# Gate of the next batch in a period's last part, slots at its end, statistics behind VectorE's chain, no adds between the dispatch scatters

## The reference

```
scores = softmax(x @ gate_w.T) + gate_b           # 16 experts in 4 groups of 4
keep the 2 groups with the largest sum of their 2 best scores
idx = the 2 best experts in these groups;  weights = softmax values at idx
y = sum over the 2 of weight * ((silu(x We1 + be1) * (x We3 + be3)) We2 + be2)
```

## Time and profile before

| | |
|---|---|
| time, three runs | 1450.14, 1455.86, 1465.67 us; median 1455.86 |
| profiled execution | 1444.71 us; span from first to last instruction 1443.0 us |
| mean granted TensorE clock | 0.943 |
| TensorE busy | 1248.3 us (87%) |
| VectorE busy | 923.5 us (64%) |
| GpSimd busy | 698.3 us (48%) |
| ScalarE busy | 668.2 us (46%) |
| chain that ended last | PE 67%, DVE 11%, issue 7%, ACT 5%, DMA 4%, another core or an unknown queue 3%, POOL 3% |

### The profile page before, as it was taken

How to read it: one execution, slowest core, us unless ns; L and a number is a source line. 1 busy time by engine, 2 the same in 40 slices (tenths; PEclk the granted TensorE clock), 3 DMA queues, 4 the chain that set the end, 5 groups by cost and what they waited for, 6 DMA issues and landing times.

```text
span 1443.0 us, 27088 instructions
## 1 busy us (share of the span) xinstructions
PE 1248.3 (87%) x7150; PEld 991.9 (69%) x7150; DVE 923.5 (64%) x3310; ACT 668.2 (46%) x1466; POOL 698.3 (48%) x848
## 2 busy tenths in 40 slices
PE   4998999899999877999999988979869999999830
PEld 3566665699998756878878874646535899998720
DVE  4674856377876556667766646756734677775556
ACT  3344431477776523344434434434411777775500
POOL 2456766488887430000000003467664688885400
PEclk9997999999999997999999998999989999999965
DMA  9521224555554423111110001122224555554389
GB/s 360 184 72 71 78 86 124 156 159 164 158 161 131 131 90 105 59 60 59 58 48 28 1 0 38 56 86 79 71 90 126 149 161 161 159 158 123 92 325 374
DMA packets 92938, 172.78 MB, mean 120 GB/s; under 512 B 17368, under 2 KB 60141, under 8 KB 91507
## 3 DMA queue, kind: packets, MB, share of 16 engines
q1 hardware_dynamic: 63318, 92.98, 21.7%
q0 software_dynamic: 26016, 67.81, 13.2%
q10 hardware_dynamic: 3456, 10.25, 1.8%
HBM read 88.51 MB, written 86.39 MB: 121 GB/s over the span
## 4 chain that ended last, share of the span: by engine, by line
PE 67%; DVE 11%; issue 7%; ACT 5%; DMA 4%; another core or an unknown queue 3%; POOL 3%; SPq 0%; DVEq 0%; ACTq 0%; POOLq 0%
PE bank L576 18%; PE bank L586 9%; PE bank L444 8%; PE bank L460 6%; PE bank L567 4%; PE bank L620 4%; PE bank L609 4%; PE bank L421 3%; PE bank L683 3%; DMA w<-routed_rows 3%; POOL expert_rows L1388 2%; PE bank L588 2%; PE bank L411 2%; ACT xn L853 1%
## 5 line engine op out<-in xcount | busy, mean ns | idle before, releaser
L1416 POOL DMA_INDIRECT routed_rows<-xn,rdest x286 | 282.9, 989 | 137.0 <-DVE rw L1213 77.3
L576 PE MATMUL bank<-rows,att 128*128 128x128 f32 x2288 | 306.8, 278 | 0.1
L576 PEld LDWEIGHTS bank<-rows,att 128*128 128x128 f32 x2288 | 282.4, 194 | 0.8 <-ACT att L841 0.4
L1388 POOL DMA_INDIRECT expert_rows<-rows,slots x192 | 186.9, 974 | 176.2 <-DVE slots L1005 110.3
L1224 DVE SCALAR_TENSOR_TENSOR rows<-bank,tile_b,att 128x128 f32<-128x128 f32 x286 | 100.1, 350 | 155.5 <-ACT att L846 121.3
L841 ACT COPY att<-w 128x512 f32 x286 | 177.9, 622 | 23.2 <-issue 16.5
L586 PE MATMUL bank<-w,rows 128*128 x572 | 173.3, 385 | 16.4 <-DVE rows L1224 15.4
L460 PE MATMUL bank<-ws,work 128*128 128x256 f32 x512 | 143.6, 424 | 25.3 <-DVE work L1135 15.5
L840 ACT COPY rows<-bank 128x256 f32<-128x256 f32 x286 | 106.7, 373 | 78.3 <-PE bank L567 57.8
L460 PEld LDWEIGHTS bank<-ws,work 128*128 128x128 f32 x512 | 103.2, 211 | 53.9 <-DVE work L1135 20.2
L1375 POOL TENSOR_TENSOR rstd<-ve,minus_half 128x8 f32<-128x8 f32 x8 | 13.1, 1640 | 257.3 <-DVE ve L965 257.3
(11 more groups left out here) (184 smaller groups left out, 2185.6 us busy)
## 6 DMA issues: line engine op xcount, KB each, us to landing
rows<-expert_rows SPq DMA_DIRECT2D x286, 130.5 KB
rows<-routed_rows SPq DMA_DIRECT2D x32, 512.0 KB, 4.2
w<-routed_rows SPq DMA_DIRECT2D x10, 1024.0 KB, 18.6
out<-xres ACTq DMA_DIRECT2D x16, 512.0 KB, 7.2
xres<-in_x SPq DMA_DIRECT2D x7, 1024.0 KB, 9.4
rows<-routed_rows SPq DMA_DIRECT2D x6, 1024.0 KB, 15.2
expert_rows<-pad SPq DMA_DIRECT2D x47, 130.5 KB
routed_rows<-xn,rdest POOLq DMA_INDIRECT x286
```

The lines of the kernel that those rows point to most:

```text
L576: last = nc.tensor.matmul(rh_ps[t % RB][:, n * P:(n + 1) * P], m.rw13[:, t % RB, c * C + n * INTER:c * C + (n + 1) * INTER], m.rT[:, t % R ...
L1388: nc.gpsimd.indirect_dma_start(out=d.xg, out_offset=bass.IndirectOffsetOnAxis(ap=m.slots[:, b % XS, k, i:i + 1], axis=0), in_=xs[:, i, :], ...
L1416: nc.gpsimd.indirect_dma_start(out=d.yt, out_offset=bass.IndirectOffsetOnAxis(ap=m.rdest[:, n:n + 1], axis=0), in_=m.ry[:, n, :], in_offse ...
```

## The change

`FIRST` becomes (0, 2, 7, 12, 17, 22, 27, 32, 37): period 0 has two parts, each later one five. The gates of batch r + 1 stand in the last part of period b (behind part 1 for period 0), and the rank matmuls of batch r in the middle of that part. The transposes move up: one in the period's second part, two in the third, one in the fourth. The gates wait for the transposed half they read instead of for both. VectorE's chain stands first in the period, the statistics of batch r + 2 behind it, then slots of batch r, the last part's work, and `negate_mean(r + 2)`. ScalarE makes the exponentials before it normalises. GpSimd makes no add among the dispatch scatters and no longer waits for `y_added` there; `rstd(r + 3)` stands behind both scatters, except `rstd(10)` in layer 1's first period. All 128 adds of a layer follow the DMAs of tiles 0 to 127 in the expert stage.

```diff
-FIRST = (0, 5, 9, 14, 18, 23, 27, 32, 37)
+FIRST = (0, 2, 7, 12, 17, 22, 27, 32, 37)
...
-BIAS_PARTS = [(b, i, c) for b in reversed(range(BATCHES)) for i in range(NT) for c in (0, P)
-              if b >= BATCHES - 2 or i >= 4 or c]
...
                 if i == 0:
-                    pe.wait_ge(s.xT_copied, 4 * r + 4)
                     wait(pe, s.shift_ready, r)
+                if i % PAIRS == 0:
+                    pe.wait_ge(s.xT_copied, 4 * r + 2 + 2 * (i // PAIRS))
...
                     if b == 0:
                         if L == 0:
                             gate_tiles(r, range(NT))
-                        shared(L, n)
-                        shared(L, n + 1)
+                        shared(L, 0)
+                        shared(L, 1)
                         for j in range(4):
                             transpose(r + 1, j)
                         rank(r)
-                        for j in range(n + 2, FIRST[1]):
-                            shared(L, j)
+                        gate_tiles(r + 1, range(NT))
                         continue
-                    shared(L, n, gate_pair)
-                    shared(L, n + 1)
-                    shared(L, n + 2, first_half)
-                    shared(L, n + 3, second_half)
-                    if n + 4 < FIRST[b + 1]:
-                        shared(L, n + 4)
-                    rank(r)
+
+                    def transposes(at):
+                        return lambda j: transpose(r + 1, at[j]) if more and j in at else None
+
+                    def gates(j):
+                        if more:
+                            gate_tiles(r + 1, (2 * j, 2 * j + 1))
+                        if j == 1:
+                            rank(r)
+
+                    n = FIRST[b]
+                    shared(L, n)
+                    shared(L, n + 1, transposes({1: 0}))
+                    shared(L, n + 2, transposes({1: 1, 3: 2}))
+                    shared(L, n + 3, transposes({1: 3}))
+                    shared(L, n + 4, gates)
...
-                    if more:
+                    if b == 0:
                         normalise(r + 1)
-                    if b == 0:
                         exponentials(r)
...
+                    exponentials(r)
+                    if more:
+                        normalise(r + 1)
                     shared(L, n)
-                    exponentials(r)
                     shared(L, n + 1)
...
-                    if n + 4 < FIRST[b + 1]:
-                        shared(L, n + 4)
                     meta(r)
+                    shared(L, n + 4)
...
             def route_work(r):
                 b = r % BATCHES
-                if b > 1:
-                    yield from slots(r - 1)
-                if b + 2 < BATCHES and r != BATCHES:
+                if r == 0:
                     yield from stats_work(r + 2)
...
-                if b + 2 < BATCHES and r != BATCHES:
+                if r == 0:
                     negate_mean(r + 2)
-                yield
+                elif b + 2 < BATCHES and b:
+                    yield from stats_work(r + 2)
...
                         if L:
                             for _ in stats_work(r + 2):
                                 pass
-                        for j in range(n + 2, FIRST[1]):
-                            shared(L, j, iter(()), 0)
                         if L:
                             negate_mean(r + 2)
                         continue
-                    shared(L, n, work, (3 if b > 1 else 0) + (5 if b + 2 < BATCHES else 0) + 1)
-                    others = FIRST[b + 1] - n - 1
-                    for j in range(others):
-                        shared(L, n + 1 + j, work, 17 // others + 1)
+                    shared(L, n, work, 6)
+                    for j in range(1, 4):
+                        shared(L, n + j, work, 5)
                     for _ in work:
                         pass
+                    for _ in slots(r):
+                        pass
+                    shared(L, n + 4, iter(()), 0)
+                    if b + 2 < BATCHES:
+                        negate_mean(r + 2)
...
                 xs = m.xs[b % XS]
-                if b >= 2 and k == 0:
-                    pool.wait_ge(s.y_added, PAIRS * (r - 1))
...
-                    if b >= 2 and i % 4 == 3:
-                        add_bias((b - 2, 2 * k + i // 4, 0))
...
                     if r == BATCHES:
                         rstd(r + 2)
-                    elif b + 3 < BATCHES:
+                    scatter(r, 1)
+                    if b + 3 < BATCHES:
                         rstd(r + 3)
-                    scatter(r, 1)
-                    if r == BATCHES:
-                        rstd(r + 3)
+
+            def add_bias(L, i):
+                if i >= 2 * NT * BATCHES:
+                    return
+                if i == 0:
+                    pool.wait_ge(s.y_added, PAIRS * (BATCHES * L + 7))
+                b, j = (BATCHES - 1 + i // (2 * NT)) % BATCHES, i % (2 * NT)
...
+                if i in (2 * NT - 1, 2 * NT * BATCHES - 1):
+                    last.then_inc(s.bias_added, 1)
```

More of the change, by code:

```diff
@@ L508, in route @@
                     more = b + 1 < BATCHES
-                    def gate_pair(j):
-                        gate(r, 2 * j)
-                        gate(r, 2 * j + 1)
-                    def first_half(j):
-                        if more and j % 2 == 0:
-                            transpose(r + 1, j // 2)
-                    def second_half(j):
-                        if more and j % 2 == 0:
-                            transpose(r + 1, 2 + j // 2)
-                    n = FIRST[b]
                     if b == 0:
@@ L1081, in route_work @@
                 yield
-                if b + 2 < BATCHES and r != BATCHES:
+                if r == 0:
                     negate_mean(r + 2)
-                yield
+                elif b + 2 < BATCHES and b:
+                    yield from stats_work(r + 2)
             def table_work(L):
-                yield from slots(BATCHES * L + BATCHES - 1)
                 nc.vector.tensor_copy(m.pad_to[:], m.carry[:]).then_inc(s.pads_ready, 1)
@@ L1375, in a_rstd @@
                 nc.gpsimd.tensor_tensor(m.rstd[:], m.ve[:], m.minus_half[:], ALU.pow).then_inc(s.a_rstd_ready, 1)
-            def add_bias(part):
-                b, i, c = part
-                x = m.xres[:, b, i, c:c + P]
-                return nc.gpsimd.tensor_tensor(x, x, m.half_bs2[:, c:c + P], ALU.add)
             def scatter(r, k):
@@ L1402, in route @@
                         rstd(r + 2)
-                    elif b + 3 < BATCHES:
+                    scatter(r, 1)
+                    if b + 3 < BATCHES:
                         rstd(r + 3)
-                    scatter(r, 1)
-                    if r == BATCHES:
-                        rstd(r + 3)
+            def add_bias(L, i):
[4 more added lines that the diff above has]
+                b, j = (BATCHES - 1 + i // (2 * NT)) % BATCHES, i % (2 * NT)
+                c = j % 2 * P
+                x = m.xres[:, b, j // 2, c:c + P]
+                last = nc.gpsimd.tensor_tensor(x, x, m.half_bs2[:, c:c + P], ALU.add)
+                if i in (2 * NT - 1, 2 * NT * BATCHES - 1):
+                    last.then_inc(s.bias_added, 1)
             def experts(L):
@@ L1419, in experts @@
                         bounds_check=last_row, oob_is_err=False).then_inc(s.rows_out[n], 16)
-                    if i == 0:
-                        pool.wait_ge(s.y_added, PAIRS * (BATCHES * L + 7))
-                    if i < len(BIAS_PARTS):
-                        last = add_bias(BIAS_PARTS[i])
-                    if i in (2 * NT - 1, len(BIAS_PARTS) - 1):
-                        last.then_inc(s.bias_added, 1)
+                    add_bias(L, i)
             ch.did(nc.gpsimd.memset(m.minus_half[:], -0.5))
```

## The result

Against the kernel before, in runs on the same chip, the changed kernel took **1539.4 us (1535.8 to 1544.0) against 1459.5 us (1450.1 to 1465.7): ratio 1.056, 95% interval 1.049 to 1.063**. The forecast was 1427, its range 1392 to 1464. The profiled execution took 1537.7 us. Later the same two kernels ran on a chip of a second kind, and there the answer turns over: 1363.5 against 1380.4 us, ratio 0.989 (0.985 to 0.992), a small gain but clear of the noise. Both results are read here. I call the chips late and clean, for what their traces show.

A forecast was written before the change was run, and what follows sets the result against it. The prediction took TensorE as the bound, with 72.6 us lost to waits and late signals in the two routing stretches. Terms -5.3 - 30.1 + 7 + 12 - 12.7 = -29.1 us, from 1455.9, gave 1427 us, range 1392 to 1464.

The forecast's parts named there:

- the burst, "+12": Dispatch scatters without adds between them: 1.0 us more for each of 12 periods, +12 us, bounds 0 and 63.
- my rival "bursts": Scatters of batches 1 to 6, run without pauses, go slower and cause lateness: +63 us, 1490 us in all, chance 0.13.
- The rank wait, -5.3: Routing stretches: TensorE's wait for VectorE's `sel` before the rank matmuls goes, -5.3 us, bounds -6.8 and 0.
- ScalarE's wait for the scatters, -30.1: Routing stretches: ScalarE's six waits before normalise for scatters freeing the xs buffer vanish, -30.1 us, bounds 0 and -30.1.
- The first period of layer 1, +7: Layer 1's first routing period: VectorE stands still until rstd(10), TensorE runs dry behind it, +7 us, bounds 0 and 11.6.
- Experts' stage, -12.7: Expert stage: 24 more adds a layer move 24 tiles from slow to quick pace, -12.7 us, bounds 0 and -12.7.
- Statistics hidden, 1.3 us to spare: Routing periods: GpSimd needs 21.8 us up to rstd, the period is at least 23.1, so waiting for rstd costs nothing.
- Adds against VectorE, 0: Expert stage: the moved adds do not hold up VectorE's scaling of the expert's output, priced at 0.
- the rival: Port conflict: the 48 moved adds stop VectorE in the expert stage and tiles gain nothing, +6.2, 1462 us, chance 0.04.
- The baseline: Both routing stretches, 191.6 us each undisturbed, lost 72.6 us together, all that a change of order can win.

The follow-up runs named there:

- a_pause8: The changed kernel with one unused GpSimd pow of 128x8 (1.66 us) between the two halves of each batch's 16 scatters: 1422.8 us, ratio 0.981, late chip.
- b_spread: The kernel before with GpSimd's new program plus a pow of 128x2 behind each batch's 4th, 8th and 12th scatter: 1404.1 us, ratio 1.017, clean chip.
- a_spread_again: The changed kernel with three pows of 128x2 a batch and pows behind the experts' last 15 scatters, rerun on a clean chip: 1389.8 us, ratio 1.007.
- a_adds4: The changed kernel with the add after every fourth dispatch scatter and the old number of adds in the experts' stage put back: 1464.5 us, ratio 1.009, late chip.
- b_gpsimd_new: The kernel before with GpSimd's part of the diff alone: 1506.4 us, ratio 1.039 on a late chip; 1372.8 us, 0.993 on a clean one.
- a_short8: The changed kernel with one pow of 128x2 (0.73 us) behind the eighth scatter of a batch: 1363.4 us, ratio 0.988, clean chip.
- a_two: The changed kernel with two pows of 128x2, behind the 5th and 10th scatter of a batch: 1365.7 us, ratio 0.990, clean chip.
- a_even: The changed kernel with an add of 128x64 on scratch behind every dispatch scatter: 1393.0 us, ratio 1.009, clean chip.

## Why the prediction was wrong

**The step that failed is the burst, "+12".** Three kernels ran on both kinds of chip. The changed kernel's span is 175.8 us longer on the late one (1536.0 - 1360.2), 8.4 of it in the experts' stages, 167 outside them. The kernel before is 64.6 us longer (1443.0 - 1378.4), 24.2 of it in the experts' stages, 40 outside. The kernel before with GpSimd's part of the change is 132.5 us longer (1501.3 - 1368.8), 8.6 in the experts' stages, 124 outside. So lateness outside the experts' stages grew by 127 us, where I had 12 with an upper bound of 63: 84 of it come with GpSimd's part in the old order, and 43 more only with the new order on top.

The mistake is in the choice of rows. I priced a run without a pause by batch 1, whose run rstd divides into eight and eight. a_pause8 is just that case, and the step is true of it: it took 1422.8. "The trace has such runs in batch 1 only" was wrong as well. The wait of 13.63 us that I quoted from layer 1's period 3 stands in a longer one, of the kernel before:

```profile
935.64 1.13 POOL L1388 DMA_INDIRECT expert_rows<-rows,slots  x1 [0.20 <-issue]
...
944.66 0.96 POOL L1388 DMA_INDIRECT expert_rows<-rows,slots  x1 [0.30 <-issue]
945.92 0.96 POOL L1388 DMA_INDIRECT expert_rows<-att,slots  x1 [0.30 <-issue]
...
949.72 0.96 POOL L1388 DMA_INDIRECT expert_rows<-att,slots  x1 [0.30 <-issue]
950.70 0.47 POOL L1380 TENSOR_TENSOR xres<-xres,half_bs 128x128 f32<-128x128 f32 x1
```

Eight scatters of batch 1 and four of batch 2 follow without a break. The gates ended at 948.1, on the tenth, and VectorE noticed 12.4 us later. That was the row for a long run: 12.4 us is near what each full period of the changed kernel lost on the late chip (36.5 against 24.0). As bound I took the pace of the experts' scatters, and my rival "bursts" looked for slower scatters, 1.81 us and more apart. Its mechanism came, its sign was right at a chance of 0.12; its place was wrong. GpSimd stays at 1.26 us, and the price is paid by ScalarE and VectorE, which wait for TensorE's signals.

The other steps:

- *The rank wait, -5.3.* Gone: one wait of 0.95 us for `sel` is left, on both kinds of chip. On a clean one the kernel before waits 8.7 us so, in five waits.
- *ScalarE's wait for the scatters, -30.1.* The waits are gone as said, on both kinds of chip; on a clean one the kernel before waits 42.5 us so. But their worth was overstated. All the new order is worth 7 to 9 us there, with the next step and the longer clean period in it. The terms that bear on a clean chip add up to -5.3 - 30.1 + 7 = -28.4; the whole change measured -16.9, with GpSimd's part in it. My bound "0 if TensorE never felt it" was nearer. The order's worth hangs on GpSimd's program, though: with three pows a batch it is some 31 us (b_spread 1404.1 against a_spread_again 1389.8 less 17.2 for its tail), where VectorE in the old order waits 73.9 us for rstd. What ScalarE's wait costs by itself no run shows.
- *The first period of layer 1, +7.* It came. VectorE waited 8.96 us for rstd, TensorE behind it 3.70 and 1.41 us:

```profile
936.07 0.17 DVE L955 TENSOR_SCALAR ve<-mv 128x8 f32<-128x8 f32 x1
945.19 0.17 DVE L967 SCALAR_TENSOR_TENSOR nmr<-mv,rstd 128x8 f32<-128x8 f32 x1 [8.96 <-POOL rstd L1358]
```

  That interval is 36.6 us, 12.6 over the 24.0 of a clean period; before it was 35.8, 5.8 over 30.0. The difference is 6.8. On clean chips it is 36.5 against 33.8, 8.7 by the same account. My own working gave 904 - 896 = 8, not the 7 that I wrote.
- *Experts' stage, -12.7.* Right on a late chip (24 x 0.52 is 12.5, a slip), from first to last scatter:

```profile
338.28 1.00 POOL L1406 DMA_INDIRECT routed_rows<-xn,rdest  x1 [25.14 <-DVE rw L1202]
...
576.01 0.97 POOL L1406 DMA_INDIRECT routed_rows<-xn,rdest  x1 [0.30 <-issue]
...
1227.49 1.00 POOL L1406 DMA_INDIRECT routed_rows<-xn,rdest  x1 [26.97 <-DVE rw L1202]
...
1465.19 0.97 POOL L1406 DMA_INDIRECT routed_rows<-xn,rdest  x1 [0.30 <-issue]
```

  237.7 us in both layers, against 525.57 - 280.31 = 245.3 and 246.2 before (the first scatter of layer 1 stands at 1127.36): 16 us. On clean chips both kernels take 233.6, whatever the number of adds:

```profile
254.13 1.00 POOL L1406 DMA_INDIRECT routed_rows<-xn,rdest  x1 [15.66 <-DVE rw L1202]
...
487.65 0.97 POOL L1406 DMA_INDIRECT routed_rows<-xn,rdest  x1 [0.30 <-issue]
```

  The 1.66 against 1.91 us of the earlier trace rows was lateness as well, and only that.
- *Statistics hidden, 1.3 us to spare.* On a clean chip rstd waits 0.67 us for `ve` and nobody behind it does: hidden, with less to spare. The clean period is 24.0 us, 1 over the undisturbed one before, which I had at 0.
- *Adds against VectorE, 0.* Line 1224 takes 135.8 / 286 = 475 ns, as before. The rule of the Trainium skill that I weighed (Advanced Engine Details and Errata, VectorE Performance Modes), that the two engines block each other at a shared port, is not put to the test here: the same section wants both tensors of such a VectorE instruction in SBUF, and line 1224 reads a PSUM bank. Nor did the row that I held against the rival, whose line reads a PSUM bank too.
- *The baseline.* "That is all that a change of order can win here", 72.6 us: on the clean chip the same two stretches take 208.0 and 208.9 us, 33.7 over the 2 x 191.6. The other 38.9 us are the late chip's, and were sensitive to something that I had not counted as part of the order, GpSimd's rests.

**What stays open.** That breaks cure most of the stall on late chips is shown by undoing (a_adds4), by adding (a_pause8) and by taking them from the kernel before (b_gpsimd_new). How much break is needed is not: a_short8, a_two and a_even never met a late chip. That the chip decides, rather than something else that differed between the comparisons, is argued and not shown: it rests on three comparisons that met lateness and three on two other chips that did not, and no chip was seen in both states. What is late inside the chip no trace shows. The moved data show nothing of it: in the stall GpSimd's queue runs at a steady rate and ends with the scatters (core 0's windows; columns as in the earlier trace rows):

```profile
126.00:130.00 4.00, 3.75 (x13) 1.73 (x12) 3.59 (x15) 3.98 (x10) 3.09 (x4) 1.00 0.28 100
134.00:138.00 4.00, 0.94 (x3) 0.11 (x1) 1.96 (x8) 0.69 (x1) 2.88 (x3) 1.00 0.28 100
138.00:142.00 4.00, 0.00 (x0) 0.00 (x0) 0.94 (x3) 0.00 (x0) 2.88 (x3) 0.74 0.28 100
146.00:150.00 4.00, 4.00 (x13) 3.17 (x13) 0.42 (x1) 0.58 (x1) 0.00 (x0) 0.50 0.00 0
```

The last columns are the granted clock, the DMA share and GB/s: 100 GB/s before and in the stall, and 104 to 118 in the like period on the clean chip. The clock falls to 0.50, the 1.2 GHz level, behind TensorE's 10 us of rest and prices the stall a second time. The Trainium skill (Perfetto Trace Analysis, DMA Instruction — SWDGE (GPSIMD)) says that the end which a trace gives for such a scatter is that of writing its descriptors, and that moving the data and the semaphore's increment come behind it. So the 0.96 us of a scatter would not show a backlog behind it; but the late signals found here are TensorE's and VectorE's, and no run looks further.

## What to carry to other kernels

Before a small instruction between GpSimd's scatters is taken away as idle time, look for waits that end by "remote", above all where an engine waits for itself: then the break may be worth more than the work (here 1.6 us of it saved up to 12 us a period). To price a run without a break, take rows without a break, and look for them across the borders of the batches. And a stall that no releaser explains may differ from chip to chip: time both kernels on more than one chip, since here the same change reads 1.056 on one and 0.989 on another; no kernel of this study is shown to be the best on both.

## What the runs showed of the hardware

- On the late chips TensorE's signals to ScalarE and VectorE come up to 13 us late from about the seventh scatter of an unbroken run on, with scatters 1.26 to 1.28 us apart; VectorE's signals to itself come about 0.4 us late from the eleventh, a few by 2 us. TensorE's few waits in such stretches are on time. The run counts across batches.
- With 0.66 us of rest in every four scatters (1409.6 us), or 1.6 us after eight (1422.8), most of it goes; a memset of 0.12 us behind each helps little (1513.0). At some 1.67 us apart, as with the adds in the experts' stage, over a hundred go with little lateness: 237.7 us in place of 233.6.
- On the clean chips the same programs have no such wait at all: the kernel before takes 1380 us against 1448 to 1460, the changed one 1363 against 1539.
- GpSimd starts a memset of 0.12 us in the 0.30 us gap between two scatters, and the next scatter keeps its pace. A pow of 128x2 takes 0.73 us, of 128x8 1.66.
